# A post-norm attention layer and a top-2 expert layer on one core: the last chunk of experts in an earlier place, put-aside sums in two buffers, and one transpose for each half of x

## The reference

```python
x = _layernorm(x + _L0_attn_ref(x, L0_attn_w_qkv, L0_attn_w_out, L0_attn_b_out), axis=-1)
x = _layernorm(x + _L0_ffn_ref(x, L0_ffn_in_proj_w, ...), axis=-1)
```

```python
        v2 = k2
        sim = jnp.einsum('bwid,bwjd->bwij', q, k2) * scale
        sim = jnp.where(mask[None, None], mask_value, sim)
        attn = jax.nn.softmax(sim, axis=-1)
        out = jnp.einsum('bwij,bwjd->bwid', attn, v2)
```

```python
        x1 = _layer_norm(x + attn_out, ln1_w, ln1_b)
        gates = jax.nn.softmax(x1 @ gate_w.T + gate_b, axis=-1)
        _, top_idx = jax.lax.top_k(gates, TOP_K)
        expert_outputs = jnp.einsum('bsd,efd->bsef', x1, expert_w) + expert_b[None, None]
        moe_out = jnp.sum(sel * top_gates[..., None], axis=2)
        return _layer_norm(x1 + moe_out, ln2_w, ln2_b)
```

## Time and profile before

| | us |
|---|---|
| median of three runs (1422.62 to 1425.06) | 1423.48 |
| the profiled execution | 1425.19 |
| its span, first to last instruction | 1423.5 |
| PE busy in it | 1334.6 (94%) |
| DVE busy | 1072.4 (75%) |
| ACT busy | 805.4 (57%) |
| POOL busy | 572.1 (40%) |

### The profile page before, as it was taken

How to read it: one execution, slowest core, us unless ns; L and a number is a source line. 1 busy time by engine, 2 the same in 40 slices (tenths; PEclk the granted TensorE clock), 3 DMA queues, 4 the chain that set the end, 5 groups by cost and what they waited for, 6 DMA issues and landing times. The chain is left out here.

```text
span 1423.5 us, 29390 instructions
## 1 busy us (share of the span) xinstructions
PE 1334.6 (94%) x9678; PEld 766.4 (54%) x9678; DVE 1072.4 (75%) x2782; ACT 805.4 (57%) x1749; POOL 572.1 (40%) x806
## 2 busy tenths in 40 slices
PE   8889899999999999999979888999999999999984
PEld 6767655545554453556656545665433445665441
DVE  3665877987888977674559977786999886666776
ACT  3235366556666567676745455656656666666541
POOL 4434422221221532223558645343454023322786
PEclk9999999999999999999989999999989999999996
DMA  3765432232111423445375543554432123443331
GB/s 113 191 179 130 123 79 62 62 91 57 40 40 47 95 58 92 110 117 147 89 181 135 133 85 74 163 166 136 109 77 63 29 48 67 131 125 104 89 73 46
DMA packets 221665, 140.77 MB, mean 99 GB/s; under 512 B 130246, under 2 KB 215934, under 8 KB 221259
## 3 DMA queue, kind: packets, MB, share of 16 engines
q1 hardware_dynamic: 209755, 123.50, 32.7%
q0 software_dynamic: 11760, 15.40, 5.6%
HBM read 97.35 MB, written 40.88 MB: 97 GB/s over the span
## 5 line engine op out<-in xcount | busy, mean ns | idle before, releaser
L1320 DVE TENSOR_REDUCE mxs<-bank 128x1 f32<-128x512 f32 (+3 forms) x1120 | 712.5, 667 | 169.2 <-PE bank L1753 95.6
L1213 ACT ACTIVATE pbuf<-bank 128x512 f32<-128x512 f32 (+1 forms) x1112 | 599.0, 593 | 296.3 <-PE bank L1804 187.7
L1781 PE MATMUL bank<-qs,ks 99*128 99x256 bf16 (+3 forms) x1536 | 426.5, 321 | 16.4 <-DVE rD L1445 6.8
L1753 PE MATMUL bank<-ks,qs 96*128 96x512 bf16 (+3 forms) x1280 | 423.3, 351 | 4.0 <-DVE mxs L1320 1.3
L1804 PE MATMUL bank<-pbuf,vcur 128*17 128x256 f32 (+3 forms) x3072 | 274.0, 474 | 9.1 <-DMA vcur<-v_scratch 7.0
L1781 PEld LDWEIGHTS bank<-qs,ks 99*128 99x128 bf16 x1536 | 142.2, 98 | 192.0 <-issue 69.4
L1753 PEld LDWEIGHTS bank<-ks,qs 96*128 96x128 bf16 x1280 | 123.1, 98 | 111.3 <-issue 21.3
L1804 PEld LDWEIGHTS bank<-pbuf,vcur 128*17 128x17 f32 x3072 | 70.8, 97 | 140.1 <-issue 97.4
L1125 POOL DMA_INDIRECT gathering<-x_scratch,gathering x69 | 68.3, 990 | 182.1 <-PE bank L1928 158.5
L1136 POOL DMA_INDIRECT gathering<-ys_scratch,gathering x48 | 78.8, 1641 | 46.9 <-issue 18.1
L1079 POOL CAST parts<-qkf 128x512 bf16<-128x512 f32 x28 | 17.7, 632 | 175.3 <-DVE qkf L1414 175.2
(11 more groups left out here) (334 smaller groups left out, 1941.6 us busy)
## 6 DMA issues: line engine op xcount, KB each, us to landing
gathering<-exp_t SPq DMA_DIRECT2D x69, 256.0 KB
vcur<-v_scratch SPq DMA_DIRECT2D x92, 136.0 KB, 2.8
parts_scratch<-parts SPq DMA_DIRECT2D x29, 384.0 KB, 3.4
ys_scratch<-gathering SPq DMA_DIRECT2D x69, 128.0 KB, 3.2
xw<-windows SPq DMA_DIRECT2D x29, 256.0 KB, 3.4
x_scratch<-x SPq DMA_DIRECT2D x53, 128.0 KB, 2.4
qs<-parts_scratch SPq DMA_DIRECT2D x32, 192.0 KB, 3.8
ks<-parts_scratch SPq DMA_DIRECT2D x28, 192.0 KB, 3.8
```

What stands on the lines that cost most here:

```text
L1213: nc.scalar.activation(pbuf[:, u0:u0 + heads, nj * P - cols:nj * P], bk[:, 0:heads * cols].rearrange("p (h t) -> p h t", h=heads), ACT.Exp)\
L1320: v.reduce_max(mxs[:, j * HJ + h:j * HJ + h + heads, c], bk[:, 0:heads * cols].rearrange("p (h t) -> p h t", h=heads), AX_X)\
L1753: last = mm(bk[:, x * cols:(x + 1) * cols].rearrange("p (n t) -> p n t", t=P), qs6[0:KR, pos % QRING, head // HJ, j, head % HJ, :], ks5[0: ...
L1781: last = mm(bk[:, x * cols:(x + 1) * cols].rearrange("p (n t) -> p n t", t=P), ks5[0:KR + NPART, kslot, kb % GT, head, :], qs6[0:KR + NPAR ...
```

## The change

Four edits, and the list of steps that `plan` makes of them:

1. `a_xT` transposes a tile of x alone (two transposes in place of four), and `a_xTc` copies it to the second half of xT. A new step `a_xP` on POOL fills the first half: zeros for the first tile of a sequence, otherwise a copy of the second half as the tile before left it. `a_s` and, where buffers are shared, `a_xTc` wait for it.
2. `f_acc0` of the first 24 tiles writes to two buffers by turns (acc[0] and x0f[0]) with a semaphore each, and no more to rD. `d_res` no longer waits for the store of the sum; `f_acc0` of tile T waits for the store of tile T-2. `d_aff` still waits for the store of x1.
3. For the last chunk the ranks of sorting, blocks, gathers and last norms are about four tiles lower.
4. In the plan a step of SP no longer waits for the landing of the one of its name before it. With this the four first tiles of x come ahead of most weights.

```diff
-        add("a_xT", T, "PE", 430, ("load_x", T), ("a_s", o))
-        add("a_xTc", T, "ACT", 495, ("a_xT", T))
+        add("a_xT", T, "PE", 215, ("load_x", T), ("a_s", o))
+
+        add("a_xP", T, "POOL", 500, *[("a_xTc", T - 1)] * (T % TB > 0), ("a_s", o))
+        add("a_xTc", T, "ACT", 280, ("a_xT", T), *[("a_xP", o + 1)] * (o >= 0))
...
-        add("a_s", T, "PE", 920, ("a_qc", T))
+        add("a_s", T, "PE", 920, ("a_qc", T), ("a_xP", T))
...
-        add("d_res", T, "DVE", 330, ("d_o", T), ("d_xb", T), ("d_aff", l), *[("f_st", l)] * (l < SPARSE))
+        add("d_res", T, "DVE", 330, ("d_o", T), ("d_xb", T), ("d_aff", l))
...
-            add("f_acc0", T, "DVE", 330, ("f_b", T), ("d_aff", T))
+            add("f_acc0", T, "DVE", 330, ("f_b", T), ("d_aff", T), ("f_st", T - 2))
...
-            back = c * CHUNK + CHUNK - 1 + 6 + 1.2 + (2.6 + 0.5 * i if c < CHUNKS - 1 else 1.3 + 0.25 * i)
+            back = c * CHUNK + CHUNK - 1 + 6 + 1.2 + (2.6 + 0.5 * i if c < CHUNKS - 1 else -2.5 + 0.25 * i)
...
-                base = last + 6 + 1.2
+                base = last + 6 + (1.2 if c < CHUNKS - 1 else -3)
...
-            ready[x] = max(ready[x], done + SETTLE[engine] + 90 * (rows[x][0] == engine and engine in ("DVE", "POOL")))
+            landed = done + SETTLE[engine] + 90 * (rows[x][0] == engine and engine in ("DVE", "POOL"))
+            ready[x] = max(ready[x], clock[engine] if (step, x) in in_turn else landed)
...
+        aside = acc[0], x0f[0]
...
-                    sp.dma_start(acc_dram[T * P:(T + 1) * P, :], rD[0]).then_inc(acc_stored, 16)
+                    sp.dma_start(acc_dram[T * P:(T + 1) * P, :], aside[T % 2]).then_inc(acc_stored[T % 2], 16)
...
+                elif name == "a_xP":
+                    if o >= 0:
+                        pool.wait_ge(*fill("a_s", o))
+                    if T % TB == 0:
+                        pool.memset(xT[e][:, :, 0:P], 0.0).then_inc(xP_ready, 1)
+                    else:
+                        pool.wait_ge(*drain("a_xT", T - 1))
+                        pool.tensor_copy(xT[e][:, :, 0:P], xT[early_set(T - 1)][:, :, P:2 * P]).then_inc(xP_ready, 1)
...
-                        if l < SPARSE:
-                            dve.wait_ge(acc_stored, 16 * (l + 1))
...
-                        v.tensor_tensor(rD[f], bk[:, 0:E], x1[f], ALU.add).then_inc(emptied[b], 1)
+                        if T >= 2:
+                            dve.wait_ge(acc_stored[T % 2], 16 * (T // 2))
+                        v.tensor_tensor(aside[T % 2], bk[:, 0:E], x1[f], ALU.add).then_inc(emptied[b], 1)
...
                     for c in range(EC):
-                        for w in range(2):
-                            last = tr(bk[:, (2 * c + w) * P:(2 * c + w + 1) * P], xw[e][:, w, c * P:(c + 1) * P],
-                                      idf[:, :])
+                        last = tr(bk[:, c * P:(c + 1) * P], xw[e][:, 1, c * P:(c + 1) * P], idf[:, :])
```

More of the change, by code:

```diff
@@ L224, in stage_steps @@
     add("ones", 0, "SP", 500, ("w_rows", 0))
-    add("ones_later", 0, "SP", 500, ("w_rows", 0), *[(x, GT - 1) for x in ("st0", "pst", "vstore", "kst2", "qst2")])
+    add("ones_later", 0, "SP", 500, ("w_rows", 0), ("a_xP", LEAD), *[(x, GT - 1) for x in ("st0", "pst", "vstore", "kst2", "qst2")])
     add("w_rows", 0, "DVE", 1500)
@@ L374, in stage_steps @@
             continue
-        add("f_acc0", T, "DVE", 330, ("f_b", T), ("d_aff", T), ("g_aff2", m))
+        add("f_acc0", T, "DVE", 330, ("f_b", T), ("d_aff", T), ("g_aff2", m), *[("f_st", T - 2)] * (T == SPARSE))
         add("f_e0", T, "PE", 1720, ("d_x1Tc", T), ("f_b", T - 1))
@@ L386, in stage_steps @@
         add("f_es", T, "POOL", 700, ("f_e3a", T))
-        add("g_load", T, "SP", 450, ("st0", tile), ("g_store", m), *alt)
+        add("g_load", T, "SP", 450, ("st0", tile), ("g_store", m), *[("f_st", T - 1)] * (T == SPARSE), *alt)
         add("g_xb", T, "POOL", 700, ("g_load", T), ("load_b2", 0))
@@ L440, in job_steps @@
             rows["ex", J, i] = ("ACT", heads * cols * 0.833 + 68, r + length * i / n,
-                                [("st", J, i)] + back + [("st0", 1), ("r_vst", 1)] * (J == i == 0))
+                                [("st", J, i)] + back + [("st0", 1), ("r_vst", 1), ("a_xP", 2)] * (J == i == 0))
         for kb in range(nk):
@@ L467, in plan @@
     rows = {step: list(row) for step, row in (*stage_steps().items(), *job_steps().items())}
-    previous = {}
+    previous, in_turn = {}, set()
     for step in sorted(rows, key=lambda x: (x[0], x[1:])):
         if step[0] in previous:
+            if rows[step][0] == "SP" and previous[step[0]] not in rows[step][3]:
+                in_turn.add((previous[step[0]], step))
             rows[step][3] = rows[step][3] + [previous[step[0]]]
@@ L785, in build @@
             sem(x) for x in ("tab_step", "x1_stored", "ids_stored", "ids_loaded"))
-        acc_stored = sem("acc_stored")
+        acc_stored = [sem(f"acc_stored{i}") for i in range(2)]
         wslot_loaded, xslot_loaded, yslot_stored = (
@@ L895, in _ @@
                 elif name == "ones_later":
+                    sp.wait_ge(xP_ready, LEAD + 1)
                     for x in range(LEAD):
@@ L991, in _ @@
                             sp.wait_ge(out_stored[f], 16 * dense_count(l))
+                        if T == SPARSE:
+                            sp.wait_ge(acc_stored[1], 16 * (SPARSE // 2))
                         sp.dma_start(x0f[f], x0_dram[tile * P:(tile + 1) * P, :]).then_inc(x0f_loaded[f], 16)
@@ L1209, in _ @@
                         act.wait_ge(x0_stored[1], 16)
+                        act.wait_ge(xP_ready, 3)
                         act.wait_ge(*drain("r_v", 1))
@@ L1236, in _ @@
                     act.wait_ge(*fill("a_xT", T))
-                    copy(xT[e], bk[:, :].rearrange("p (c t) -> p c t", c=EC)).then_inc(emptied[b], 1)
+                    if o >= 0:
+                        act.wait_ge(xP_ready, o + 2)
+                    copy(xT[e][:, :, P:2 * P], bk[:, 0:E].rearrange("p (c t) -> p c t", c=EC)).then_inc(emptied[b], 1)
                 elif name == "a_qc":
@@ L1556, in _ @@
                         dve.wait_ge(z_ready, l - SPARSE + 1)
+                    if T == SPARSE:
+                        dve.wait_ge(acc_stored[0], 16 * (SPARSE // 2))
                     v.tensor_tensor(acc[f], bk[:, 0:E], x1[f], ALU.add).then_inc(emptied[b], 1)
@@ L1839, in _ @@
                     pe.wait_ge(*drain("a_q", T))
+                    pe.wait_ge(xP_ready, T + 1)
                     for c in range(EC):
```

9 lines of the change are left out of this document (4 added, 5 removed).

## The result

The changed kernel takes 1415.44 us (median of 4, 1412.66 to 1415.98) against 1424.27 for the kernel before (median of 4): a ratio of 0.9939 with a 95% interval of 0.9916 to 0.9962. It is 9 us faster, where 21.5 were forecast. The time lies in the forecast range, but the gain is under half of what the sum said, so at least one of its terms is wrong. The profiled execution took 1415.87, its span is 1414.0.

The account below looks back on a forecast made before the run. PE, busy 1334.6 of 1423.5 us, was taken as the bound. The terms sum to -21.7 us, taking the profiled 1425.2 to 1403.5; the median being 1.7 lower gives 1402 us, range 1389 to 1417.

Parts of the forecast that it names:

- Transposes, -7.0: PE, first two thirds: two fewer transposes for each of 32 tiles, 0.22 us per tile, counted whole; -4 to -9.
- Case B: Stalls of the new order: a load in SP's queue, a store awaited by d_aff, low clock; +9, 1411 us, chance 0.17.
- C: Both old stalls go and the tail is short, with 2 us more of clock; -11, 1391 us, chance 0.11.
- Copies on POOL, 0: POOL: fills and copies of 0.4 us each, 10 to 23 us in all, done in time; 0 to +3.
- Two buffers, -1.7: Tile 17: d_res stops waiting for the sum's store, d_aff then waits for the x1 store; stall shrinks 1.7 us.
- My bound of -6.8: Tile 17: low side of the two-buffer term, PE's whole 6.8 us wait gone if the store lands sooner.
- SP's plan, -6.5: Job 21: value load issued 4.0 us sooner, stall 5.8 shorter, clock 1.3, less 0.6 for h_load; 0 to -9.6.
- Last chunk, -7.5: Tail: last chunk's work moved ahead; 2.3 + 2.5 + 1.3 + 1.4 us saved, between -3 and -13.
- the gate's wait: Tile 30's gate, 1381.0 to 1389.1 us, with 3.9 us of standing PE: -1.3 within the last-chunk term.
- The quarter of the 5.4 us after 1300: PE's idle time between 1300 and 1365.5 us: a quarter saved, -1.4 within the last-chunk term.
- Start, -2: Before 55.4 us: x of tiles 1 to 3 ahead of output weights trims 10.1 us idle; +3 to -5.
- A new order's stalls, +3: Whole kernel: all rows move and the new list may have stalls of its own; 0 to +15.

Follow-up runs that it names:

- the second profile: Another profiled execution of the changed kernel, nothing altered: span 1412.0 us, with 40.7 us of PE's work at half clock.
- The run with late copies: Kernel before with the transposes halved and POOL copies added, old step list kept, each copy no earlier than its tile's a_xT: 1428.85 us, ratio 1.0031.
- edit 1 with early copies: Kernel before with the transposes halved and POOL copies added, old step list kept, each copy as early as it may: 1427.80 us, ratio 1.0017.

## Why the prediction was right and wrong

**Transposes, -7.0: wrong, and the largest miss.** The work went (64 rows fewer), the time did not: with the list kept, +0.17% for leaving them out and nothing for putting them back. The step that failed is "where PE is mostly the full one, and I count it whole". I read 49.9 of 50 us busy as the pace of PE. The busy rows can't say that: matmuls overlap (rows of 0.38 us start 0.22 apart), and a wait of a tenth or two of a us behind one doesn't open a gap. PE's steps pass waits for DVE's maxima, their store and ACT's copies at each job, and a PE that comes 0.22 us sooner gives part of it back at the next of them, as at 376 us above, and the rest further on. That it goes so at every job is argued from the places above, not counted. The bound of -4 that I gave for a slower pace was not wide enough either; it should have reached 0. That busy time fell by 6.1, near 7.0, is chance: 9.1 us of slower clock are in it.

**The clock: a term that the sum does not have.** The prediction counts the granted clock at job 21 alone (and 2 us in cases B and C) and puts it at nothing elsewhere. How much it matters shows in 29 executions of the kernel before, in one group of runs: the six with a granted clock of 0.979 or 0.980 took 1420.7 to 1424.1 us, the four at 0.973 or 0.974 took 1427.8 to 1429.5. Before, PE works 38.8 us of the profiled execution at half clock, in the changed kernel 57.0. Worked out from the mean granted clocks, less the last stretch where PE does nothing, the changed kernel loses some 5 to 8 us more by it than before. That is an estimate, and it overlaps with the terms above and below, since such a stretch mostly begins in or behind a stop or a string of small waits, as at 44.5, 303.9, 730.6, 764.7 and 853.5 us. It is not shown that the clock alone explains the miss: the second profile has 1.8 us more of PE's work at half clock than before, and is 11.5 us faster and not 21.5.

**Copies on POOL, 0: right.** In the changed kernel they take 0.40 us in the median and 0.43 in the mean, and nobody waits for one:

```profile
L1064 POOL COPY xT<-xT 128x256 f32<-128x256 f32 x26 | 11.2, 432 | 15.5 <-PE bank L1864 15.4
```

(The 15.4 us are POOL's own idle time before them.) The run with late copies shows that the cover is the list's: six waits, 13.4 us of ACT, and 0.31% slower. POOL's busy time rose by 8.1 us, a little less than the 10 to 20 named.

**Two buffers, -1.7: mechanism and place right, size wrong.** `d_aff` waits for the x1 store as forecast, but 8.0 us and not 5. DVE was there at 848.4, not 851, as the sum came 1.8 us sooner and the rows behind it took no longer than before; the store was issued one us sooner only, took 11.1 us to land and not 9.7, and so landed at 856.3, not 855.9. So the term was +1.3 in the changed kernel's stop (8.1 against 6.8). Taking the whole edit, it is worth most of the change: alone it gave 11 us, with the list kept 5.0. My bound of -6.8 was that of the stop alone. On the rule that I weighed (the Trainium skill, DMA: Bandwidth & Descriptors, section Queues, rings and completion order): it says that an increment lands only behind all earlier writes of that DMA engine. The trace agrees so far as it goes: with the second buffer and semaphore the store took 11.1 us to land, 9.7 without. No run shows the order of writes itself. What the edit did was to let DVE pass `d_res`; where the new list puts the next step that needs the store behind its landing, the stop is gone.

**SP's plan, -6.5: most of the stop went, the gain did not stay.** PE stopped 2.56 us where it had stopped 6.98, 4.4 us less and not 5.8. Its `pv` of job 21 came at 731.5, not 737.1, and the clock did not stay up: from 731.5 to 737.3 it was 0.50, with PE busy for 5.78 of 5.80 us, so the 1.3 us for it did not come either. The load's issue:

```profile
727.87 0.54 SPq L974 DMA_DIRECT2D vcur<-v_scratch  x1
```

But the lead of 7.8 us at 757 us was 2.1 by 794. In between lie 6.9 us at half clock (the row of 764.70 above, the 1.2 GHz level with PE busy throughout, so 3.4 us), which before has not; ahead of it, from 760.0, PE was busy for 3.0 of 4.7 us, before for 3.7. Where the other 2.3 us went was not followed. The step that failed is the one that took PE's releaser for the whole cause. Two other waits on the same queue ran beside it; with the value load alone moved nothing changed, and with two loads moved the stop was still 4.6 us.

**Last chunk, -7.5: nearly right.** The last stretch went from 18.8 to 13.4 us (-5.4, forecast 4.8), the gate's wait from 3.9 to 2.6 (-1.3, forecast 1.3); alone the edit gave 5.7 us of median. The quarter of the 5.4 us after 1300 did not come: the stretch has 4.4 us of idle time in 61 and DVE is at 51.1. PE in the gate's place, against the earlier trace rows:

```profile
1385.98 0.27 PE L1929 MATMUL bank<-idb,wpad 128*128 128x128 bf16 x1 [2.63 <-DVE wpad L1556]
```

**Start, -2: wrong.** The lead of 2.4 us at 35 us was gone at 74. x of the fourth tile came sooner, but PE then stood 3.9 us for POOL's `r_rope` of tile 3, and the clock was at its half level there. Up to 96 us PE worked 16.5 us at half clock, before 8.6:

```profile
46.16 1.09 PE L1888 MATMUL bank<-idf,ks 128*128 128x128 f32 x4 [3.94 <-POOL ks L1091]
```

```profile
44.50:51.40 6.90, 4.46 (x20) 4.12 (x21) 1.63 (x4) 0.60 (x1) 4.50 (x7) 0.51 0.82 202
```

**A new order's stalls, +3: not to be told apart.** What the new list's own stops cost can't be separated from what the other terms gave back. Case B named the two kinds, its sign came (a single wait of PE over 5 us, the 8.1 at tile 17), and its 1411 is nearest of the five. Its sum is off: two stops of 7 us less the 3 counted, and 2 of clock, are 13 and not 9, so 1415, and that this meets the measured time is luck, since the load stuck in SP's queue cost 2.56 us and not 7. B took the stops for bad luck of a list; one of them, the store at `d_aff`, was there to be reckoned at full length.

By places, the 9.5 us between the spans are these: nothing up to 1311 us, where the lead is -0.6; 4.7 us from there to PE's last matmul; 5.4 in the last stretch. Of the terms that lay ahead of 1311 us (transposes, sums, SP's plan, start: 17.2 us), none had arrived there in sum.

## What to carry to other kernels

"PE 99% busy" says that PE has no gaps, not that it sets the pace: before counting work taken off it, check what it waits for at the next few hand-overs, and give 0 as one bound. Compare PE's busy time only together with the granted clock: 9 us of it were clock here. A stop of 7 us is worth its length only if nothing else is late at the same time, so read what every other engine waited for in the same stretch, and follow each to its queue; here three waits on one queue lay side by side, and PE's list named one. When an edit frees a resource, look for the next step that needs the same transfer and where the new list puts it: in the changed list two buffers for one of two stores moved the stop and two buffers for both removed it, while in two other lists the first were enough.

## What was not expected

- A 128 KB store took 9.7 us to land in one list and 11.1 and 12.1 in two executions of the next, issued at nearly the same place; the median of the changed kernel's 24 x1 stores is 2.8 us.
- Transposes left out of a list that is kept brought nothing (+0.17%), transposes added to one cost 0.34%.
- Single executions of one kernel differ by more than the effects of the smaller edits: 12 runs of edit 1 with early copies went from 1422.3 to 1430.9. A good part of it goes with the granted clock, as the 29 executions above show. A profile of one execution can carry a place and a mechanism, not a gain of 3 us.
- In one group of runs all kernels were slow, before by 2.4%, at a mean granted clock of 0.964 to 0.966. Its profiles have stops of PE of 3 to 12 us around 500 and 860 us and between 1165 and 1210 that the others don't have, each while the indirect stores of a sorting step (`t_sc`) ran or just behind them. Their cause was not looked for.
